# Layer 0, first batch: reciprocals for the memory's queries move to unit 1, the memory's products to units 2 and 3, and all the bit work on the codes' second half to unit 0

## The chip, the cores and the metric

The kernel runs on one core of a Trainium2 chip. The metric is the device time of one execution in microseconds (us); the median of several runs stands for a kernel. The engines have one instruction queue each and meet only at semaphores: PE (TensorE), DVE (VectorE), ACT (ScalarE), POOL (GpSimd) and SP (SyncE, which issues all the DMAs here).

## The reference, cut to what matters

Two layers; each adds an attention block and a feed-forward block to the residual `x` of shape (8, 256, 256). The change lies in layer 0, in its first two batches of eight. Layer 0's attention is a softmax attention with 32 query heads on 8 key heads, plus a read of a small fixed memory by transformed queries:

```
xn      = layernorm(x)
q, k, v = xn @ Wq.T, xn @ Wk.T, xn @ Wv.T
a_dot   = softmax(q k^T / sqrt(8)) v
sigma_q = elu(q)                                     # 4 query groups of 64 numbers per token
a_mem   = sigma_q @ memory / (sigma_q @ memory_norm)
w       = sigmoid(memory_weight)
x       = x + a_dot * (1 - w) + a_mem * w + ffn(xn)
ffn(xn) = (gelu(xn @ Wg.T) * (xn @ Wu.T)) @ Wd.T     # Wg, Wu, Wd: 4-bit codes times block scales, 2048 wide
```

The 4-bit weights are decoded on the chip. A byte with two codes is turned by shifts and masks into two bytes that are read as 8-bit floats (the "bits" below); those are multiplied with the scales, and the product is split into a high and a low part for the matmuls.

## The kernel before, in words

**Units.** Layer 0 runs as a software pipeline of units `u` from -3 (`FIRST`) on, one for each of the 64 pairs of batch and key head. Every engine walks the same list of units, and within one does, in a fixed order, its share of: the turned scores and exponentials of attention unit u, the scores and row maxima of unit u+2, the weighted values of unit u-1, the feed-forward gate and up products of m = u-1 (one of eight pieces `a` of the hidden width), and the down product of m-2. The dictionary that `schedule()` returns puts further steps of a batch (its statistics, normalisation, projections, the memory's read) at given units. All engines read the same dictionary, so moving an entry moves the step on every engine that has a part in it.

**The steps touched.** `recip0` and `recip1` make 1/(1 - tanh) parts of the elu for the two halves of the queries. On DVE (L602, L604): a tensor_scalar and a reciprocal into `q_rec`. On POOL (L331, L334): a product (semaphore `q_mul_done`) and a subtraction into `sigma` (`sigma_done`). `q_rec` lies in the same memory as `xn`, the normalised tokens. `norm` on DVE (L584) writes `xn` for batch b and waits, for b > 0, until `q_mul_done` has reached 2b. `mem` is the memory's read for one tile of 128 tokens: PE multiplies `sigma` with the memory (L848, waits for `sigma_done`), DVE takes a reciprocal, multiplies out of PSUM (L615, semaphore `mem_mul`) and adds to X (L618). `turn` transposes `xn` on PE (L825), ACT copies the high part (L421), DVE makes the low part (L588).

**One PSUM bank, `misc`.** The steps `turn`, `q`, `kv`, `v`, `mem` and `gamma` share it with the transposed maxima and with the weighted values. So PE's `steps(u)` waits ahead of the first step of a unit for `max_split` of unit u+1 (which DVE does in `split_max`, its first work of a unit), and between two steps of one unit for the DVE and ACT to have emptied the bank (`evicted`; for `mem` that is `mem_mul`). After its steps PE goes on, in order, with `scores_turned(u, 1)` (L891), `scores(u + 2, 0)` (L866), the up product (L794), `weighted(u - 1)` (L906), half of the down product (L933), `scores(u + 2, 1)` and `turn_out`.

**DVE's order in a unit.** split_max(u+1); the steps that don't use `misc` (stats, norm, recip); decoding of two weight pieces (L707) in units 0 to 5; the first gelu product (L755); the steps that use `misc`; maximum(u+2, 0) (L652); the second gelu product (L763); maximum(u+2, 1); normalised(u-1) (L671, L676); the low part of one weight piece (L712).

**POOL's order in a unit.** hidden_low(m-1) (L365); hidden(m) (L371), which waits for DVE's L763; weights_low(u+2) (L375), which waits for ACT's high part (L466); then the steps in the dictionary.

**Before the pipeline is full.** In unit -1 DVE does `decode(2)`, `decode(3)`, the memory's weights (L558 to L563), recip0, `weights_low(1)` and two of four bit operations on the second half of the codes (`nibble_bits(1, 0)` is L685 and L686, `nibble_bits(1, 1)` is L689); in unit 0 recip1, the statistics of batch 1 and the other two (L692, L695). The first half's bits are done with the same four calls in unit -3.


Of the kernel before, what the change touches and what calls it, by code (L numbers as in the profile page):

```python
# [75 lines left out]
def schedule():  # L76

    at = {}

    def put(u, *step):  # L80
        at.setdefault(u, []).append(step)

    for kind in ("stats", "norm", "turn", "q", "qlow", "kv", "qload0", "mask0", "qload1", "mask1"):
        put(FIRST, kind, 0)
    put(-1, "recip0", 0)
    put(0, "recip1", 0)
    put(0, "v", 0)
    put(1, "mem", 0)
    put(2, "mem", 1)
    put(GAMMA_AT, "gamma", 0)  # L90
    for b in range(1, BATCH):
        late = int(b == 1)
        for n, kind in ((0, "stats"), (1, "norm"), (2 + late, "turn"), (3 + late, "q"), (4 + late, "qlow"), (4 + late, "qload0"), (4 + late, "kv"),
                        (5, "mask0"), (5, "recip0"), (6, "recip1"), (8, "qload1"), (8, "mask1")):
            put(HEADS * (b - 1) + n, kind, b)
        for t in range(2):
            put(HEADS * (b - 1) + 7 + t, "mem", 2 * b + t)
        put(HEADS * (b - 1) + 9, "v", b)
    for b in range(BATCH):
        put(HEADS * b + HEADS + 1, "att", b)  # L100
        put(HEADS * b + HEADS + LAG + BEHIND, "mlp", b)
    return at


def layer0(nc, dram, keep):

    X, ident = keep["X"], keep["ident"]
    at = schedule()
    with ExitStack() as ctx:
        def sb(name, shape, dt=F32):  # L110
            return ctx.enter_context(nc.sbuf_tensor(name, shape, dt))
# [30 lines left out]
        stats = sb("stats0", [P, 2, 6])  # L142
# [41 lines left out]
        def w_exact(n):  # L184
            return w_stage[:] if n % 2 == 0 else hid_flat if n < 6 else low_front
# [10 lines left out]
        def attends(u):  # L196
            return 0 <= u < UNITS
# [114 lines left out]
        def _(pool):  # L312
# [55 lines left out]
            def hidden(m):  # L368
                pool.wait_ge(S["v1_done"], m + 1)
                pool.wait_ge(S["up_copied"], m + 1)  # L370
                pool.tensor_tensor(hid[:, m % 2, :], g[:, m % 2, :], hid[:, m % 2, :], ALU.mult).then_inc(S["hid_done"], 1)  # L371

            def weights_low(a):
                pool.wait_ge(S["w2_hi_done"], 2 * a + 1)
                pool.tensor_tensor(w_lo[:, a, 0, :], w_exact(2 * a), w_hi[:, a, 0, :].bitcast(F32), ALU.subtract).then_inc(S["w2_lo_even"], 1)  # L375
# [15 lines left out]
            for u in range(FIRST, LAST):  # L391
                m = u - LAG
                if 0 <= m - 1 < M:
                    hidden_low(m - 1)
                if 0 <= m < M:
                    hidden(m)
                if 0 <= u + 2 < PAIRS_N and u >= 0:
                    weights_low(u + 2)
                for kind, n in at.get(u, []):
                    if kind == "mask1" and u == FIRST:  # L400
                        weights_low(0)
                    step(kind, n)
                    if kind == "recip0" and u == -1:
                        weights_low(1)
                i, odd = divmod(u - SIGN_AT - 1, 2)
                if 0 <= i < PIECES and not odd:
                    signs(i)
                if 0 <= u - NEXT_AT - 2 < 4:
                    next_low(u - NEXT_AT - 2)
# [138 lines left out]
        def _(dve):  # L548
# [130 lines left out]
            def nibble_bits(half, n):  # L679

                at4 = slice(PAIRS_N // 2 * CW * half, PAIRS_N // 2 * CW * (half + 1))
                c, lo, hi, part = codes[half], low[:, at4], high[:, at4], bits[half]
                if n == 0:
                    dve.wait_ge(S[f"codes{half}"], 16)
                    dve.tensor_scalar(part, c, 2, 0x1C1C, ALU.logical_shift_left, ALU.bitwise_and).then_inc(S["dve_link"], 1)  # L685
                    dve.tensor_scalar(lo, c, 4, 0x8080, ALU.logical_shift_left, ALU.bitwise_and).then_inc(S["dve_link"], 1)  # L686
                    dve.wait_ge(S["dve_link"], linked(2))
                elif n == 1:
                    dve.tensor_tensor(lo, lo, part, ALU.bitwise_or).then_inc(S["dve_link"], 1)  # L689
                    dve.wait_ge(S["dve_link"], linked())  # L690
                elif n == 2:
                    dve.tensor_scalar(part, c, 2, 0x1C1C, ALU.logical_shift_right, ALU.bitwise_and).then_inc(S["dve_link"], 1)  # L692
                    dve.wait_ge(S["dve_link"], linked())
                else:
                    dve.scalar_tensor_tensor(out=hi, in0=c, scalar=0x8080, in1=part, op0=ALU.bitwise_and, op1=ALU.bitwise_or).then_inc(S["dve_link"], 1)  # L695
                    dve.wait_ge(S["dve_link"], linked())
# [13 lines left out]
            def weights_low(a):  # L710
                dve.wait_ge(S["w2_hi_done"], 2 * a + 2)
                dve.tensor_tensor(w_lo[:, a, 1, :], w_exact(2 * a + 1), w_hi[:, a, 1, :].bitcast(F32), ALU.subtract).then_inc(S["w2_lo_odd"], 1)  # L712
# [8 lines left out]
            for u in range(FIRST, LAST):  # L721
                m = u - LAG
                if u == FIRST:
                    for kind, n in at[u]:
                        if kind == "turn":
                            split_weights()
                        if kind != "kv":
                            step(kind, n)
                        if kind == "turn":
                            for k in range(4):  # L730
                                nibble_bits(0, k)
                    decode(0)
                    decode(1)
                    continue
                if attends(u + 1):
                    split_max(u + 1)
                for kind, n in at.get(u, []):
                    if kind not in FROM_MISC and u >= 0:
                        step(kind, n)
                i = u - SUM_AT  # L740
                if 0 <= i < PIECES:
                    dve.wait_ge(stage_sem[i % 2], 16 * (PAIRS_N // 2 + i // 2 + 1))
                    dve.tensor_reduce(asum[:, i:i + 1], stage[:, i % 2, 0:PIECE], AX_X, ALU.add, apply_absolute_value=True).then_inc(S["summed"], 1)
                if i == PIECES:
                    dve.wait_ge(S["summed"], PIECES)
                    dve.tensor_reduce(gsum[:], asum[:].rearrange("p (m n) -> p m n", m=3), AX_X, ALU.add).then_inc(S["summed"], 1)
                if u == 0:
                    nibble_bits(1, 2)
                    nibble_bits(1, 3)
                if 0 <= u < PAIRS_N - 2:  # L750
                    decode(2 * u + 4)
                    decode(2 * u + 5)
                if 0 <= m < M:
                    dve.wait_ge(S["sq_done"], m + 1)
                    dve.scalar_tensor_tensor(out=g[:, m % 2, :], in0=g[:, m % 2, :], scalar=1.0, in1=gate[:], op0=ALU.add, op1=ALU.mult).then_inc(S["u_done"], 1)  # L755
                for kind, n in at.get(u, []):
                    if kind in FROM_MISC:
                        step(kind, n)
                if attends(u + 2):
                    maximum(u + 2, 0)  # L760
                if 0 <= m < M:
                    dve.wait_ge(S["t_done"], m + 1)
                    dve.scalar_tensor_tensor(out=g[:, m % 2, :], in0=g[:, m % 2, :], scalar=1.0, in1=gate[:], op0=ALU.add, op1=ALU.mult).then_inc(S["v1_done"], 1)  # L763
                if attends(u + 2):
                    maximum(u + 2, 1)
                if u == FIRST + 1:
                    weights_low(0)
                if attends(u - 1):
                    normalised(u - 1)
                if u == -1:  # L770
                    decode(2)
                    decode(3)
                    memory_weights()
                    for kind, n in at[u]:
                        step(kind, n)
                    weights_low(1)
                    nibble_bits(1, 0)
                    nibble_bits(1, 1)
                if 0 <= u < PAIRS_N - 2:
                    weights_low(u + 2)  # L780
                if 0 <= u - NEXT_AT - 1 < KC:
                    next_centred(u - NEXT_AT - 1)
# [1233 lines left out]
```

## Time and profile before

| | us |
|---|---|
| median of 3 runs | 831.69 |
| lowest, highest | 831.38, 834.46 |
| the profiled execution's own time | 834.6 |
| its span, first to last instruction | 832.6 |
| mean granted TensorE clock | 0.955 |

Shares of the span that the engines are busy: PE 89%, DVE 75%, ACT 56%, POOL 51%. Layer 0 takes the first 600 us and some more, layer 1 the rest.

In the timeline a row is: start in us from the span's start, duration in us, engine, line, operation, output<-input with shapes, how many instructions were merged, and in brackets how long the engine was idle before it and who released it. A duration includes time in which the instruction was held back after its start. Ends of matmuls are modelled.

### The profile page before, as it was taken

The numbers are of one execution on the slowest core, as the hardware profiler recorded it, in microseconds if no ns is written. First come the engines' busy times: TensorE is split into PE (matmuls) and PEld (weight loads), VectorE is DVE, ScalarE is ACT, GpSimd is POOL, SyncE is SP. The second block draws the span as 40 slices with busy tenths as digits, with TensorE's granted clock in tenths as the row PEclk, the third lists the DMA queues.
The fourth block names the chain that finished last, engine by engine and source line by source line (L and its number), as shares of the span: only waits on it lengthen the run. The fifth ranks groups of instructions, "written<-read, shape, count | busy, mean of one in ns | idle before, by whom it ended". The sixth has DMA issues, their size and how long they took to land. (4 is left out here: it accounts for less than half of the span.)

```text
span 832.6 us, 15164 instructions
## 1 busy us (share of the span) xinstructions
PE 740.0 (89%) x5602; PEld 636.9 (76%) x5602; DVE 623.2 (75%) x1095; ACT 467.6 (56%) x746; POOL 424.4 (51%) x369
## 2 busy tenths in 40 slices
PE   3268799999999999999999999999977899999873
PEld 2256678888888888888888888888866677877773
DVE  6989878787687776767768777767346698999965
ACT  4246646655665665665566556657676656665410
POOL 2344354354346567757634524445627386584732
PEclk9569999999999999999999999999989999999985
DMA  5111121112011010101100000020110000000000
GB/s 159 29 40 40 39 78 37 36 48 59 2 33 33 24 46 21 48 27 40 34 3 21 20 3 21 4 96 3 58 35 0 1 1 26 1 1 26 1 26 25
DMA packets 22108, 25.89 MB, mean 31 GB/s; under 512 B 4498, under 2 KB 17170, under 8 KB 22036
## 3 DMA queue, kind: packets, MB, share of 16 engines
q1 hardware_dynamic: 22036, 24.93, 10.5%
q8 instruction: 45, 0.74, 0.4%
q14 instruction: 27, 0.22, 0.1%
HBM read 14.83 MB, written 3.28 MB: 22 GB/s over the span
## 5 line engine op out<-in xcount | busy, mean ns | idle before, releaser
L652 DVE TENSOR_REDUCE neg_max<-s_pair 128x4 f32<-128x1024 f32 x127 | 155.0, 1220 | 75.6 <-PE s_pair L866 75.3
L474 ACT ACTIVATE probs<-t_pair 128x1024 f32<-128x1024 f32 x128 | 131.2, 1025 | 136.4 <-PE t_pair L891 136.1
L371 POOL TENSOR_TENSOR hid<-g,hid 128x512 f32<-128x512 f32 x64 | 82.1, 1282 | 177.9 <-DVE g L763 144.8
L365 POOL TENSOR_TENSOR hid_lo<-hid,hid_hi 128x512 fp32r<-128x512 f32 x64 | 85.5, 1335 | 82.9 <-ACT hid_hi L497 82.8
L866 PE MATMUL s_pair<-K,Q 96*128 96x256 f32 x508 | 85.0, 291 | 15.6 <-DVE neg_max L652 9.3
L866 PEld LDWEIGHTS s_pair<-K,Q 96*128 96x128 f32 x508 | 75.8, 195 | 24.2 <-issue 8.1
L891 PE MATMUL t_pair<-Q,K 104*128 104x512 f32 x256 | 86.2, 418 | 0.3 <-DMA Q<-max_parts 0.3
L933 PE MATMUL down<-hi,hid_hi 128*128 128x256 f32 x256 | 83.9, 328 | 0.8 <-POOL hid_lo L365 0.8
L906 PE MATMUL misc<-probs,V 128*32 128x256 f32 x1024 | 69.4, 389 | 3.4 <-DVE kc L608 2.6
L933 PE MATMUL down<-lo,hid_hi 128*128 128x256 f32 x256 | 71.5, 279 | 0.0
L933 PE MATMUL down<-hi,hid_lo 128*128 128x256 f32 x256 | 71.2, 278 | 0.0
L933 PEld LDWEIGHTS down<-hi,hid_hi 128*128 128x128 f32 x256 | 48.0, 187 | 26.9 <-issue 24.7
L1124 POOL TENSOR_TENSOR rows<-rows,par 128x512 f32<-128x512 f32 x24 | 32.9, 1373 | 63.6 <-DVE rows L1598 46.5
L1770 PE MATMUL lbank<-lo,hi 128*128 128x512 f32 x192 | 51.2, 410 | 10.5 <-DVE l_hid L1569 9.3
L794 PE MATMUL gate<-xn_hi,hi 128*128 128x256 f32 x256 | 57.3, 305 | 0.0
L508 ACT ACTIVATE g<-g 128x512 f32<-128x512 f32 x64 | 40.1, 627 | 29.7 <-DVE g L755 29.7
L755 DVE SCALAR_TENSOR_TENSOR g<-g,gate 128x512 f32<-128x512 f32 x64 | 42.7, 668 | 18.0 <-ACT g L500 17.8
L1717 PE MATMUL lbank<-hi,lo 128*128 128x512 f32 (+1 forms) x192 | 51.0, 367 | 2.4 <-ACT lo L1315 2.3
L1770 PEld LDWEIGHTS lbank<-lo,hi 128*128 128x128 f32 x192 | 35.7, 193 | 22.4 <-DVE l_hid L1569 14.0
L794 PE MATMUL up<-xn_hi,hi 128*128 128x256 f32 x256 | 52.2, 286 | 0.0
L794 PE MATMUL up<-xn_lo,hi 128*128 128x256 f32 x256 | 51.9, 285 | 0.0
L794 PE MATMUL up<-xn_hi,lo 128*128 128x256 f32 x256 | 51.8, 284 | 0.0
(260 smaller groups left out, 1956.2 us busy)
## 6 DMA issues: line engine op xcount, KB each, us to landing
stage<-in_ternary SPq DMA_DIRECT2D x18, 256.0 KB, 2.8
Q<-q_hi SPq DMA_DIRECT2D x64, 64.0 KB, 2.0
stage<-in_scales SPq DMA_DIRECT2D x8, 384.0 KB, 3.4
X<-in_x SPq DMA_DIRECT2D x8, 256.0 KB, 4.2
Q<-q_lo SPq DMA_DIRECT2D x32, 64.0 KB, 2.0
Q<-max_parts SPq DMA_DIRECT2D x128, 4.0 KB
out<-X SPq DMA_DIRECT2D x8, 256.0 KB, 2.1
signs<-w_stage SPq DMA_DIRECT2D x9, 128.0 KB, 1.8
```

The lines of the kernel that those rows point to most:

```text
L365: pool.tensor_tensor(hid_lo[:, m % 2, :, :].rearrange("p a n -> p (a n)"), hid[:, m % 2, :], hid_hi[:, m % 2, :, :].rearrange("p a n -> p ...
L371: pool.tensor_tensor(hid[:, m % 2, :], g[:, m % 2, :], hid[:, m % 2, :], ALU.mult).then_inc(S["hid_done"], 1)
L474: act.activation(probs[:, u % 2, th, :], t_pair[:], ACT.Exp, scale=SCALE).then_inc(S["probs_done"], 1)
L652: dve.tensor_reduce(neg_max[:, u % 2, 4 * jp:4 * jp + 4], score_banks(u, jp)[:].rearrange("p (s n) -> p s n", n=SEQ), AX_X, ALU.max, negat ...
L755: dve.scalar_tensor_tensor(out=g[:, m % 2, :], in0=g[:, m % 2, :], scalar=1.0, in1=gate[:], op0=ALU.add, op1=ALU.mult).then_inc(S["u_done" ...
L794: mm = pe.matmul(out, lhs[a][k], rhs[b][k], start=(n == 0), stop=(n == 3 * KC - 1))
L866: mm = pe.matmul(score_banks(u, jp)[:, 512 * j + SEQ * s:512 * j + SEQ * s + SEQ], Q[0:KROWS, quad, 2 * jp + j, P * s:P * s + P], K[0:KROW ...
L891: mm = pe.matmul(t_pair[:, 512 * jp:512 * jp + 512].rearrange("p (j n) -> p j n", j=2), K[rows, quad, hq, P * th:P * th + P], Q[rows, quad ...
L906: mm = pe.matmul(misc[32 * j:32 * j + 32, 0:SEQ], V[:, th, h, :], probs[:, u % 2, th, SEQ * j:SEQ * j + SEQ], start=(th == 0), stop=(th == ...
L933: mm = pe.matmul(down[:, D * t:D * t + D], h[:, m % 2, n, P * t:P * t + P], w[:, a, n, 2 * D:3 * D], start=(a == 0 and t == 0 and n == 0 a ...
L1717: mm = pe.matmul(dst, lhs[a](k), rhs[b](k), start=(first and n == 0), stop=(last and n == 3 * KC - 1))
L1770: mm = pe.matmul(banks[bank][:], w[:, k, P * c:P * c + P], x[:, k, :], start=(n == 0), stop=(n == 3))
```

## The change

```diff
@@ schedule()
     for kind in ("stats", "norm", "turn", "q", "qlow", "kv", "qload0", "mask0", "qload1", "mask1"):
         put(FIRST, kind, 0)
-    put(-1, "recip0", 0)
-    put(0, "recip1", 0)
     put(0, "v", 0)
-    put(1, "mem", 0)
-    put(2, "mem", 1)
+    put(1, "recip0", 0)
+    put(1, "recip1", 0)
+    put(2, "mem", 0)
+    put(3, "mem", 1)
     put(GAMMA_AT, "gamma", 0)
     for b in range(1, BATCH):
         late = int(b == 1)
-        for n, kind in ((0, "stats"), (1, "norm"), (2 + late, "turn"), (3 + late, "q"), ...
+        for n, kind in ((0, "stats"), (1 + late, "norm"), (2 + late, "turn"), (3 + late, "q"), ...
@@ gpsimd
                 for kind, n in at.get(u, []):
                     if kind == "mask1" and u == FIRST:
                         weights_low(0)
                     step(kind, n)
-                    if kind == "recip0" and u == -1:
-                        weights_low(1)
+                if u == -1:
+                    weights_low(1)
@@ vector
                 if u == 0:
-                    nibble_bits(1, 2)
-                    nibble_bits(1, 3)
+                    for k in range(4):
+                        nibble_bits(1, k)
...
                     decode(2)
                     decode(3)
                     memory_weights()
-                    for kind, n in at[u]:
-                        step(kind, n)
                     weights_low(1)
-                    nibble_bits(1, 0)
-                    nibble_bits(1, 1)
```

Both halves of the reciprocals of batch 0 (DVE and POOL) now stand in unit 1, `mem` of tile 0 in unit 2, `mem` of tile 1 in unit 3 ahead of `turn` of batch 1, `norm` of batch 1 in unit 2, and DVE's four bit operations on the second half of the codes in unit 0. The set of instructions is the same.

## Rows read from the trace of the kernel before

**Rows 1.** Busy us by stage, per engine (instructions), then granted clock, DMA share, GB/s.

```profile
60.00:80.00 20.00, 15.08 (x127) 12.52 (x126) 18.74 (x27) 11.98 (x19) 10.21 (x7) 1.00 0.15 41
...
120.00:140.00 20.00, 20.00 (x178) 17.22 (x171) 15.03 (x29) 10.26 (x17) 9.14 (x8) 1.00 0.14 36
```

**Rows 2.** Waits of DVE, 20 to 90 us: total us, times, longest.

```profile
DVE neg_max L652 <- PE s_pair L866: 5.9, 6, 1.9
```

**Rows 3.** Timeline, unit -3: bits of the codes' first half, POOL idle.

```profile
9.50 0.55 DVE L685 TENSOR_SCALAR probs<-probs 128x1536 uint16<-128x1536 uint16 x1
...
10.55 0.96 DVE L689 TENSOR_TENSOR X<-X,probs 128x1536 uint16<-128x1536 uint16 x1
```

**Rows 4.** Timeline, unit -1, of DVE, ACT and POOL.

```profile
30.02 0.85 ACT L466 ACTIVATE hi<-w_stage 128x768 fp32r<-128x768 f32 x1 [6.61 <-DVE w_stage L707]
...
31.42 0.28 DVE L602 TENSOR_SCALAR xn<-queries 128x256 f32<-128x256 f32 x1
...
31.74 1.75 DVE L604 RECIPROCAL xn<-xn 128x256 f32<-128x256 f32 x1
...
33.41 0.90 DVE L712 TENSOR_TENSOR lo<-hid,hi 128x768 fp32r<-128x768 f32 x1
...
34.22 1.08 DVE L685 TENSOR_SCALAR probs<-probs 128x1536 uint16<-128x1536 uint16 x1
...
35.84 2.11 POOL L375 TENSOR_TENSOR lo<-w_stage,hi 128x768 fp32r<-128x768 f32 x1
...
36.33 2.44 DVE L689 TENSOR_TENSOR X<-X,probs 128x1536 uint16<-128x1536 uint16 x1
```

**Rows 5.** Timeline, end of unit 0 to start of unit 2.

```profile
48.22 0.73 POOL L331 TENSOR_TENSOR queries<-queries,xn 128x256 f32<-128x256 f32 x1
...
49.03 0.73 POOL L334 TENSOR_TENSOR queries<-queries 128x256 f32<-128x256 f32 x1
...
51.75 0.71 DVE L584 TENSOR_SCALAR xn<-X,mv,rstd 128x256 f32<-128x256 f32 x2
...
54.90 0.18 DVE L613 RECIPROCAL a_rec<-misc 128x4 f32<-128x4 f32 x1
...
55.92 1.22 DVE L652 TENSOR_REDUCE neg_max<-s_pair 128x4 f32<-128x1024 f32 x1
...
59.06 1.82 POOL L375 TENSOR_TENSOR lo<-w_stage,hi 128x768 fp32r<-128x768 f32 x1
...
59.48 2.22 DVE L712 TENSOR_TENSOR lo<-X,hi 128x768 fp32r<-128x768 f32 x1
...
60.84 1.98 POOL L365 TENSOR_TENSOR hid_lo<-hid,hid_hi 128x512 fp32r<-128x512 f32 x1
...
62.14 1.50 DVE L707 SCALAR_TENSOR_TENSOR w_stage<-X,stage 128x768 f32<-128x768 fp8e4 x1
...
62.26 0.71 PE L848 MATMUL misc<-mem,queries 128*128 128x130 f32 x4 [1.61 <-DVE max_parts L661]
```

**Rows 6.** Timeline, unit 3, of PE and DVE.

```profile
72.37 0.66 PE L825 MATMUL misc<-ident,xn 128*128 128x128 f32 x4 [1.61 <-DVE max_parts L661]
...
74.54 0.67 DVE L755 SCALAR_TENSOR_TENSOR g<-g,gate 128x512 f32<-128x512 f32 x1
...
75.00 0.40 PE L794 MATMUL up<-xn_lo,hi 128*128 128x256 f32 x2
...
75.87 1.07 PE L906 MATMUL misc<-probs,V 128*32 128x256 f32 x16 [0.47 <-DVE xn_lo L588]
...
78.36 1.23 DVE L652 TENSOR_REDUCE neg_max<-s_pair 128x4 f32<-128x1024 f32 x1 [0.82 <-PE s_pair L866]
```

**Rows 7.** Timeline of PE, unit 6.

```profile
107.70 0.71 PE L866 MATMUL s_pair<-K,Q 96*128 96x256 f32 x4 [1.89 <-issue]
...
110.46 1.93 PE L906 MATMUL misc<-probs,V 128*32 128x256 f32 x16
```

**Rows 8.** Windows: half a microsecond of unit 6, columns as in Rows 1.

```profile
109.50:110.00 0.50, 0.50 (x4) 0.50 (x4) 0.50 (x2) 0.00 (x0) 0.50 (x1) 0.50 0.88 309
```

More of the change, by code:

```diff
@@ L92, in schedule @@
         late = int(b == 1)
-        for n, kind in ((0, "stats"), (1, "norm"), (2 + late, "turn"), (3 + late, "q"), (4 + late, "qlow"), (4 + late, "qload0"), (4 + late, "kv"),
+        for n, kind in ((0, "stats"), (1 + late, "norm"), (2 + late, "turn"), (3 + late, "q"), (4 + late, "qlow"), (4 + late, "qload0"), (4 + late, "kv"),
                         (5, "mask0"), (5, "recip0"), (6, "recip1"), (8, "qload1"), (8, "mask1")):
```

## The prediction

> **What bounds the kernel now.** I read the busy shares by stage first, then the waits, then the timeline unit by unit. Busy time by stage [rows 1] shows two regimes: from 60 to 80 us DVE is busy 18.74 of 20 us and PE 15.08; from 120 to 140 us PE is busy for all 20.00 and DVE for 15.03. So the first units are set by DVE, later ones by PE. The waits of DVE from 20 to 90 us [rows 2] say that it stood still for 5.9 us only, each time between two row maxima that PE must serve. All engines walk the same units and are tied to each other in each, so I take it that a microsecond won or lost on DVE before unit 4 comes through to the end, one for one. The change moves work only inside units -1 to 3; I follow DVE through them.
>
> **Unit -1.** The first reciprocal step goes: from 31.42 to the end of the row that starts at 31.74 and takes 1.75 us, 2.07 us [rows 4]. Behind it stands DVE's `weights_low(1)` at 33.41. It cannot move up by as much. POOL's own `weights_low(1)` no longer waits behind its recip0 and starts when ACT has made the high part, at 30.02 + 0.85 = 30.87; it takes 1.82 us [rows 4, 5], to 32.7. Where DVE met such a POOL instruction it was held until that was over: the row at 36.33 took 2.44 us, ending 0.82 us after POOL's of 35.84 to 37.95; the same operation with POOL idle took 0.96 [rows 3, 4]. So `weights_low(1)` starts at 32.7 in place of 33.41: 0.7 us won (bounds 0.7 and 2.07).
>
> **The bits.** The first two bit operations of the second half took from 34.22 to 38.77, 4.55 us, beside POOL's recip0 and `weights_low(1)`; for the first half they took from 9.50 to 11.51, 2.01 us [rows 3, 4]. In the new unit 0 they start at some 35 us, when POOL has finished `weights_low(1)` and has nothing until the next high part. So 2.54 us are won (bounds 0 and 2.54; I take the whole). The other two cost the same where they are.
>
> The Trainium skill ("SBUF — State Buffer", Who interferes with whom) says that a VectorE instruction with two SBUF inputs and a GpSimd instruction that reads SBUF share a port, and that whoever comes first holds it for its whole length. The trace agrees: 0.82 us left after POOL's end, against 0.96 alone. By it both terms above stand as they are; it speaks against the change in unit 2 below, where four more POOL instructions come beside DVE's.
>
> **Unit 0.** The second reciprocal step goes too, 2.07 us. Split maxima of head 1 come 6 us earlier, so PE's transposes, turned scores and scores of head 2 are early, but DVE is what they wait for next, so that is worth nothing by itself. Batch 1's statistics stay. Sum to here: -0.7 - 2.5 - 2.1 = -5.3 us.
>
> **Unit 1.** Both reciprocal steps come in, +4.1 us. `norm` leaves, 51.75 to 52.39, -0.6; `mem` leaves, from 54.90 to the maximum at 55.92, -1.0 [rows 5]. DVE has no pause here that could hide them: they stand ahead of decoding, and gate, scores and up of PE are finished before DVE asks for them. SP's loads of the next scales come earlier than before and are off the path. At the end of unit 1 the new kernel is -5.3 + 4.1 - 0.6 - 1.0 = -2.8 us.
>
> **Unit 2.** This is the first place where it loses. `norm` may not write until POOL has done the product of recip1, since it writes over the reciprocals. POOL stands late: its steps come behind hidden(0), which waits for DVE's second gelu product, and behind weights_low(3). In the old times: weights_low(3) runs from 59.06 to 60.88, DVE's weights_low from 59.48, held up, to 61.70 [rows 5]. POOL's first product meets that and ends about 0.65 after it, 62.35; the next two start at the measured step of 49.03 - 48.22 = 0.81 us and end near 64.0. DVE would begin `norm` where decoding began, 62.14. It waits 1.9 us (bounds 0.5, if POOL goes ahead of DVE's weights_low, and 2.7, if it is held up twice), and `norm` itself is +0.6. The fourth POOL operation and then hidden_low(0), 1.98 us with its wait, run beside norm and two decodings; before, only the tail of hidden_low did and made one of them 1.50 us. I add 0.7 (0 to 1.3; the nearest row is that decoding at 62.14, which ran beside hidden_low until 62.82, 0.7 us). The page's rule would add 1.3, everything in turn, and make the sum 0.6 larger. PE's `mem` waits for `sigma_done`, near 65.1 in place of 62.26, but DVE has the norm and the decodings to do meanwhile; that is hidden. Sum: +3.2, the kernel stands at +0.4.
>
> **Unit 3.** Here is the largest term. PE now has two steps on `misc`: `mem` of tile 1, then `turn` of batch 1. Between them PE waits for DVE to have multiplied out of `misc`. DVE comes to that only after decoding and the first gelu product. The gelu product starts at 74.54 and ends at 75.21 [rows 6]; reciprocal and product of `mem` are 0.6 of its 1.0 us, so the bank is free at 75.75. Queued on PE behind that wait are turn, turned scores, scores of u+2 and the up product: from 72.37 to 75.40 before, 3.03 us, all of it in DVE's decoding time. Now they start at 75.75 and end at 78.8; the weighted values follow, where before they followed at 75.87 [rows 6]. Then half of down, and the scores that DVE's second maximum at 78.36 waited for already (0.82 us idle). Nothing of the 2.9 us is covered: DVE has `turn`, one maximum and one product, 2.6 us, and then stands. `mem`'s 1.0 us on DVE lies inside. +2.9 us (bounds 2.0, from the 0.82 idle and DVE's own extra 1.0, and 3.9).
>
> **TensorE's clock.** PE will stand still for some 4.4 us in unit 2 (before `mem`; it was 1.61) and for 1.6 and 2.9 us in unit 3. In unit 6 of the old trace PE was idle for 1.89 us before row 107.70, and soon after it the granted clock was 0.50, 1.2 GHz [rows 7, 8]; the weighted values then took 1.93 in place of 1.07 us [rows 6, 7]. Unit 3's chain on PE (3.0 us, and 2.5 from 75.87 to 78.36) is now on the path, so half clock in it costs: 0.9 for the weighted values alone, 5.5 if all of it ran at half clock. I take 1.5, since such a spell covered only part of unit 6. The Trainium skill ("TensorE: Matmul & The Clock Gate", Part 1) says that the clock is gated by how busy the array has been; by that rule the fall comes in both units, as by the row.
>
> **Sum.** -2.8 + 3.2 + 2.9 + 1.5 = +4.8 us. The profiled execution took 834.6 us (span 832.6), 2.9 above the median 831.69 of the runs shown, and at their top; the terms are differences of a few units and I put them on the median: 836.5 us. What a measurement of this kernel can tell from no change is about 0.5%, 4.2 us: below 827.5 and above 835.9.
>
> **Rivals.**
> - *The waits are shorter and the clock stays up.* POOL gets in ahead of DVE's weights_low, PE's gaps fall so that no half clock comes into unit 3: -2.8 + 0.6 + 0.5 + 2.0 to 2.9 + 0 = +0.3 to +1.5, about 832.9. For it: at 60 to 62 and 71 to 72 us PE was idle 1.61 us without harm [rows 5, 6]. Against: the new gaps are longer. Chance 0.3.
> - *The early start is kept* (the other side). The bits freed from POOL and PE's early start give 5.3 us before unit 1, and unit 3 refills from it: if weighted values and down in unit 3 were not what DVE waits for (it has batch 1's low part and a longer low-weights step to do), only norm's wait remains: -5.3 + 2.5 + 0.6 + 0.5 = -1.7, 830; and the half clock in unit 6, which hangs on where PE's gap falls, may vanish, up to -1.4 more by the 0.9 of one row and the 2.0 around it. It decides faster only where unit 3 adds under 1 us. Against it: PE walks in order, so 3.03 us of work is really behind `mem_mul`. Chance 0.13, of which 0.08 is beyond 0.5%.
> - *Twice held.* Half clock already in unit 2: PE's mem to up, some 3 us, doubles and pushes unit 2's weighted values behind DVE as well, +1 to +2, and most of unit 3 at half clock too, 2.9 + 4.5: -2.8 + 3.2 + 1.5 + 7.4 = +9.3, 841. Chance 0.12.
> - *The change does less than it says*: the terms cancel within a microsecond because the units before 4 leave slack later (DVE idle between maxima). Chance 0.05.
>
> The forecast has the remaining 0.4, from +3 to +7 us; three quarters of it lies above 4.2 us. Slower: 0.3 + 0.12 and some of the first rival's top, 0.48. Faster 0.08. Same 0.44. The likeliest case's own range is 834.7 to 838.7; with the others 830.5 to 840.5.
>
> **What would show it.** In the new profile: row L685 of the second half near 35 us at 0.55 us; a wait of DVE's L584 on POOL's L331 of some 1.9 us in unit 2; a wait of PE's L825 on DVE's L615 of 2 to 3 us in unit 3, and behind it a maximum L652 idle for over 2 us; half clock near 60 to 75 us. The prediction is wrong if L584 starts without a wait, if PE reaches `weighted` in unit 3 as early against DVE as before, or if a later stage gives the difference back.

## The result, and the profile after

| | median us | lowest to highest | ratio to the kernel before, 95% interval |
|---|---|---|---|
| before (6 runs beside it) | 831.6 | 831.29 to 834.46 | |
| changed (6 runs) | 837.81 | 835.91 to 840.79 | 1.0058 (1.0033 to 1.0083) |

The change costs 6.2 us by the medians; 4.8 was forecast (836.5). The ratio of the table, which is worked out from all the runs and is not the quotient of the medians, makes it 4.8 us (2.7 to 6.9). The profiled execution of the changed kernel took 840.79 us, its span is 838.8 (before 832.6).

The best ruler in both traces is DVE's first instruction of a unit, the split maximum L659. The time from one such row to the next is the length of the unit. These rows of the changed kernel open units 2, 3 and 4 (timeline, DVE):

```profile
60.65 0.27 DVE L659 CAST max_parts<-misc 8x128 fp32r<-8x128 f32 x1
...
73.99 0.27 DVE L659 CAST max_parts<-misc 8x128 fp32r<-8x128 f32 x1
...
88.74 0.27 DVE L659 CAST max_parts<-misc 8x128 fp32r<-8x128 f32 x1
```

Unit 2 is 73.99 - 60.65 = 13.34 us long, unit 3 14.75. All lengths, worked out like this from the traces:

| unit | -1 | 0 | 1 | 2 | 3 | 4 | 5 | 6 | 7 |
|---|---|---|---|---|---|---|---|---|---|
| before | 13.93 | 12.43 | 10.39 | 10.11 | 9.72 | 11.25 | 13.08 | 10.25 | 8.38 |
| changed | 8.76 | 12.54 | 12.60 | 13.34 | 14.75 | 11.25 | 13.08 | 10.22 | 8.37 |
| sum of differences | -5.17 | -5.06 | -2.85 | +0.38 | +5.41 | +5.41 | +5.41 | +5.38 | +5.37 |

So by these two traces, one execution of each kernel, the change is worth +5.4 us, all of it made in units -1 to 3 and none given back after. The rest of the 6.2 us between the two spans is not its doing: the first split maximum stands at 24.87 us before and at 26.75 after, 1.9 us later, with the same instructions ahead of it (PE's first projection started 0.6 us later, and from the start of PE's kv product to ACT's copy of it it took 3.0 us in place of 1.7, its rows 0.63 us each in place of 0.40); e5, e6, e7 and e9 below, in which that code is the same too, have it between 24.6 and 26.3; near 325 us the trace of before has half clock that the other has not, 1.5 us the other way; 0.4 us are in layer 1.

**The stage** (busy time, columns as in [rows 1]):

```profile
60.00:80.00 20.00, 12.36 (x75) 10.15 (x74) 16.48 (x26) 7.44 (x11) 9.72 (x8) 0.84 0.08 20
```

DVE is busy for 16.48 us where it was 18.74 [rows 1], PE for 12.36 in place of 15.08, and the granted clock fell from 1.00 to 0.84: both engines stand more, so it is waits that were added, not work. (The two windows hold different parts of the units, so they show the kind of the loss and not its size.)

**What DVE waits for now** (waits of DVE, 20 to 90 us, columns as in [rows 2]):

```profile
DVE neg_max L652 <- PE s_pair L862: 7.1, 6, 3.5
DVE xn L584 <- POOL queries L331: 1.7, 1, 1.7
DVE xn_lo L588 <- ACT xn_hi L421: 1.4, 1, 1.4
```

Against 5.9 us for maxima alone [rows 2] there are now 7.1, and two waits that were not there. PE's waits from 60 to 80 us name the other side:

```profile
PE misc L821 <- DVE a_mem L615: 2.7, 1, 2.7
PE misc L844 <- POOL queries L334: 2.5, 2, 1.5
```

**Units -1 and 0** (timeline, DVE and POOL; answers to [rows 3, 4]):

```profile
32.83 1.81 POOL L375 TENSOR_TENSOR lo<-w_stage,hi 128x768 fp32r<-128x768 f32 x1 [6.82 <-ACT hi L466]
...
33.10 1.61 DVE L563 TENSOR_SCALAR mem<-mem,mw 128x128 f32<-128x128 f32 x1
...
34.64 0.94 DVE L712 TENSOR_TENSOR lo<-hid,hi 128x768 fp32r<-128x768 f32 x1
...
36.95 0.53 DVE L685 TENSOR_SCALAR probs<-probs 128x1536 uint16<-128x1536 uint16 x1
...
37.98 0.96 DVE L689 TENSOR_TENSOR X<-X,probs 128x1536 uint16<-128x1536 uint16 x1
```

POOL's weights_low starts right after ACT's high part, DVE's L563 is held up by it (1.61 in place of 0.28 us) and its weights_low follows. L685 takes 0.53 and L689 0.96 us, as with POOL idle in unit -3 [rows 3]; before the change they took 1.08 and 2.44 [rows 4].

**Unit 2** (timeline, the same engines and PE; answers to [rows 5]):

```profile
59.87 1.44 POOL L331 TENSOR_TENSOR queries<-queries,xn 128x256 f32<-128x256 f32 x1
...
62.07 0.72 POOL L331 TENSOR_TENSOR queries<-queries,xn 128x256 f32<-128x256 f32 x1
...
62.26 0.46 PE L844 MATMUL misc<-mem,queries 128*128 128x130 f32 x2 [1.53 <-POOL queries L334]
...
62.90 2.13 DVE L584 TENSOR_SCALAR xn<-X,mv,rstd 128x256 f32<-128x256 f32 x2 [1.66 <-POOL queries L331]
...
63.65 0.66 PE L844 MATMUL misc<-mem,queries 128*128 128x130 f32 x2 [0.93 <-POOL queries L334]
...
64.94 0.95 DVE L707 SCALAR_TENSOR_TENSOR w_stage<-X,stage 128x768 f32<-128x768 fp8e4 x1
...
70.34 1.23 DVE L652 TENSOR_REDUCE neg_max<-s_pair 128x4 f32<-128x1024 f32 x1 [0.24 <-PE s_pair L862]
```

DVE's `norm` at 62.90 has waited 1.66 us for POOL's second product, and takes 2.13 us for its two instructions (0.71 before), held up by POOL's fourth operation and by hidden_low. PE's two products for `mem` come at 62.26 and 63.65, waiting for `sigma_done`. The granted clock is at its lower level from 63.8 to 67.3 us, but DVE's second maximum waits for only 0.24 us, so the end of this unit is DVE's.

**Unit 3** (timeline of PE and DVE; answers to [rows 6]):

```profile
74.62 0.71 PE L844 MATMUL misc<-mem,queries 128*128 128x130 f32 x4 [1.61 <-DVE max_parts L661]
...
77.59 0.42 DVE L615 TENSOR_TENSOR a_mem<-misc,a_rec 128x256 f32<-128x256 f32 x1
...
78.07 1.12 PE L821 MATMUL misc<-ident,xn 128*128 128x128 f32 x4 [2.73 <-DVE a_mem L615]
...
82.83 0.63 PE L790 MATMUL up<-xn_lo,hi 128*128 128x256 f32 x2
...
83.39 1.50 PE L902 MATMUL misc<-probs,V 128*32 128x256 f32 x16
...
86.29 1.22 DVE L652 TENSOR_REDUCE neg_max<-s_pair 128x4 f32<-128x1024 f32 x1 [3.53 <-PE s_pair L862]
```

PE does `mem` at 74.62 and stands for 2.73 us until DVE has multiplied out of the bank (77.59 + 0.42). Turn to the end of up takes from 78.07 to 83.46, 5.4 us in place of 3.03, since the granted clock is at its lower level, 1.2 GHz, from 77.5 to 84.3 us. A row of the windows within it (columns as in [rows 1]):

```profile
78.50:79.00 0.50, 0.50 (x5) 0.50 (x4) 0.00 (x0) 0.00 (x0) 0.00 (x0) 0.50 0.00 0
```

The weighted values follow at 83.39 and DVE's second maximum at 86.29, after an idle time of 3.53 us (0.82 before).

### The profile page after: what moved, and what is told of

Same layout as the page of the kernel before. It is cut to its first block and busy times, and to the rows that moved or that the text cites. A ratio compares the mean times of both kernels' runs of the same rounds, so it can differ in the third digit from the quotient of the medians.

```text
span 838.8 us, 15164 instructions
## 1 busy us (share of the span) xinstructions
PE 748.1 (89%) x5602; PEld 644.5 (77%) x5602; DVE 621.9 (74%) x1095; ACT 468.3 (56%) x746; POOL 424.9 (51%) x369
## 5 line engine op out<-in xcount | busy, mean ns | idle before, releaser
L862 PE MATMUL s_pair<-K,Q 96*128 96x256 f32 x508 | 86.8, 295 | 17.9 <-DVE neg_max L652 12.5
L862 PEld LDWEIGHTS s_pair<-K,Q 96*128 96x128 f32 x508 | 77.7, 199 | 26.8 <-DVE neg_max L652 8.8
```

Source lines behind the costliest of these rows:

```text
L862: mm = pe.matmul(score_banks(u, jp)[:, 512 * j + SEQ * s:512 * j + SEQ * s + SEQ], Q[0:KROWS, quad, 2 * jp + j, P * s:P * s + P], K[0:KROW ...
```

## The experiments

For each run the unit lengths come from its trace; each is from one traced execution. They agree between traces to 0.05 us wherever the code is the same and no spell of half clock lies differently (it does in unit 3, table behind e5, and in units 5 and 6), so they tell more than the whole times, of which one kernel's lie up to 6 us apart. The kernel before had a median of 832.62 us beside e1 to e4, 833.57 beside e5 to e8 and 833.45 beside e9. In the diffs "..." stands for lines left out.

| | units -1, 0, 1, 2, 3 | sum of 5 | median us | ratio to before, 95% |
|---|---|---|---|---|
| before | 13.93, 12.43, 10.39, 10.11, 9.72 | 56.6 | | |
| changed | 8.76, 12.54, 12.60, 13.34, 14.75 | 62.0 | 837.81 | 1.0058 (1.0033 to 1.0083) |
| e1 mem in the down bank | 8.75, 12.54, 12.61, 13.38, 10.74 | 58.0 | 834.16 | 1.0021 (1.0007 to 1.0034) |
| e2 filler in unit 3 | 8.76, 12.54, 12.60, 13.36, 11.97 | 59.2 | 837.34 | 1.0049 (1.0032 to 1.0065) |
| e3 mem first | 8.76, 12.53, 12.61, 13.36, 11.43 | 58.7 | 835.37 | 1.0029 (1.0012 to 1.0046) |
| e4 own reciprocals | 8.75, 12.54, 12.59, 13.86, 14.18 | 61.9 | 837.38 | 1.0059 (1.0036 to 1.0083) |
| e5 mem late | 13.92, 12.42, 9.39, 10.11, 14.03 | 59.9 | 837.30 | 1.0045 (1.0029 to 1.0062) |
| e6 bits | 9.35, 14.50, 10.39, 10.12, 9.72 | 54.1 | 831.12 | 0.9970 (0.9955 to 0.9985) |
| e7 gaps | 9.42, 14.30, 10.84, 10.12, 9.72 | 54.4 | 831.75 | 0.9974 (0.9961 to 0.9988) |
| e8 own reciprocals, filler | 8.76, 12.54, 12.60, 11.71, 13.61 | 59.2 | 836.01 (1 run) | |
| e9 bits, first in the pause | 9.43, 13.43, 10.40, 10.13, 9.70 | 53.1 | 830.73 | 0.9966 (0.9948 to 0.9983) |

The ratios to the kernel before agree with the sums to 0.7 us, but for e2: +4.1 us (2.7 to 5.4) by its ratio, +2.6 by its trace.

### e1: the memory's products in another bank

```diff
 # PE, step "mem"
+                    if b == 1:
+                        pe.wait_ge(S["mem_mul"], 1)
-                        mm = pe.matmul(misc[:, ...
+                        mm = pe.matmul((down if b < 2 else misc)[:, ...
 # PE, evicted
-                elif kind == "mem":
+                elif kind == "mem" and n >= 2:
 # PE, down_product
+                    if m == 0:
+                        pe.wait_ge(S["mem_mul"], 2)
 # DVE, step "mem"
-                    am = misc[:, ...
+                    am = (down if b < 2 else misc)[:, ...
```

> The changed kernel, but the memory's two products of batch 0 go to the PSUM bank of the down product (unused until the end of unit 3), so PE need not wait for DVE between them and turn in unit 3. The unit lengths here are from one first split-maximum row (L659) to the next. Theory (the wait for the shared bank is the cost): unit 3 falls from 14.75 to some 10.7 us, that is the 9.72 of the kernel before and 1.0 for the step on DVE; whole time 4 us below the changed kernel. Rival A (half clock is the cost, the wait is not): unit 3 stays over 12.7. Rival B (DVE's added work is the cost): unit 3 stays at 13.7 or more.

Unit 3 took 10.74 us. The timeline of PE and DVE:

```profile
74.82 0.60 PE L821 MATMUL misc<-ident,xn 128*128 128x128 f32 x4
...
78.78 1.07 PE L904 MATMUL misc<-probs,V 128*32 128x256 f32 x16 [0.97 <-DVE xn_lo L588]
...
81.26 1.23 DVE L652 TENSOR_REDUCE neg_max<-s_pair 128x4 f32<-128x1024 f32 x1 [0.81 <-PE s_pair L864]
```

Turn follows `mem` at once, at full clock, and the whole queue behind it goes by while DVE decodes. The weighted values now wait for DVE's low part of batch 1, as before the change; what is left of unit 3 is DVE's own 1.0 us. Rival B falls: of the 5.03 us that unit 3 had gained, 4.0 hang on the shared bank. Rival A's number did not come either, but with the wait the half clock is gone too (the granted clock is 1.00 from 73.6 to 84.4 us), so what each is worth is left to e2. The run shows one thing more: here the granted clock was 0.50 up to 69.2 us, through most of unit 2, and that unit took 13.38 us where the changed kernel with its shorter spell took 13.34. Half clock costs nothing there.

### e2: the same wait, with the clock held up

```diff
                     if before:
+                        if u == 3:
+                            for n3 in range(20):
+                                pe.matmul(down[:, 0:SEQ], w_hi[:, 0, 0, 0:P], xn_hi[:, 0, 0, :], start=True, stop=True)
                         evicted(*before)
```

> The changed kernel with 20 useless matmuls of 256 columns on PE in unit 3, between the memory's product and the wait for the bank, into the still unused down bank; they take some 2.4 us of a wait of 2.73. Theory (2.0 of the 5.0 us of unit 3 are half clock after PE's pause): the granted clock stays 1.0 and unit 3 falls from 14.75 to 12.7 us. Rival (the clock costs nothing on the path): unit 3 stays at 14.7 or grows.

Unit 3 took 11.97 us, 2.8 less than without the filler; 12.7 was expected. The timeline:

```profile
74.23 2.64 PE L944 MATMUL down<-xn_hi,hi 128*128 128x256 f32 x20
...
77.22 0.66 PE L821 MATMUL misc<-ident,xn 128*128 128x128 f32 x4 [0.35 <-DVE a_mem L615]
...
80.19 1.07 PE L902 MATMUL misc<-probs,V 128*32 128x256 f32 x16
...
82.68 1.23 DVE L652 TENSOR_REDUCE neg_max<-s_pair 128x4 f32<-128x1024 f32 x1 [1.73 <-PE s_pair L862]
...
84.19 0.98 DVE L712 TENSOR_TENSOR lo<-X,hi 128x768 fp32r<-128x768 f32 x1
```

The last of these in the kernel before:

```profile
79.88 1.65 DVE L712 TENSOR_TENSOR lo<-X,hi 128x768 fp32r<-128x768 f32 x1
```

Turn begins as late against the unit's start as before (77.22 - 73.12 = 4.10, in the changed kernel 78.07 - 73.99 = 4.08), but the queue behind it is through in 2.97 us, not 5.32. DVE's second maximum stands 9.56 us into the unit (82.68 - 73.12); it was 6.63 before the change (78.36 - 71.73) and 12.30 with it (86.29 - 73.99). So up to there the queue behind the bank is worth 2.93 us and half clock 2.74. Behind it the changed kernel is 0.64 us and this one 0.68 us quicker than the kernel before: DVE's weights_low came clear of POOL's and took 0.98 us here in place of 1.65. That makes 2.93 + 2.74 - 0.64 = 5.03. The 2.93 hold the 1.0 us of DVE's own step, which e1 left in the unit. The whole times do not show the gain (837.34 us beside 837.81 for the changed kernel), and this is one trace; the table behind e5 bears it out from four others.

### e3: DVE empties the bank first

```diff
+                if u == 3:
+                    step("mem", 1)
                 if 0 <= u < PAIRS_N - 2:
                     decode(2 * u + 4)
...
-                    if kind in FROM_MISC:
+                    if kind in FROM_MISC and (u, kind) != (3, "mem"):
```

> The changed kernel, but in unit 3 DVE does its part of the memory's read for tile 1 ahead of decoding instead of after the first gelu product. Theory (PE's queue behind the bank is the cost, since DVE comes late): PE's turn starts 2 us earlier against the start of the unit, and unit 3 takes about 11.8 us in place of 14.75. Rival (DVE's order is of no account since DVE does the same work): 14 us or more, with a new wait of DVE for PE's product.

```profile
74.44 0.18 DVE L613 RECIPROCAL a_rec<-misc 128x4 f32<-128x4 f32 x1 [0.81 <-PE misc L846]
...
75.14 1.12 PE L823 MATMUL misc<-ident,xn 128*128 128x128 f32 x4 [0.74 <-DVE a_mem L615]
...
79.57 1.07 PE L904 MATMUL misc<-probs,V 128*32 128x256 f32 x16
```

Turn starts 75.14 - 73.05 = 2.09 us into the unit in place of 4.08, at the price of 0.81 us in which DVE waits for PE's product. Unit 3 took 11.43 us; 11.8 was expected. Part of it ran at half clock still (L823 1.12 us).

### e4: norm without its wait

```diff
+        q_rec0 = hid[:, 1, :].rearrange("p (c n) -> p c n", c=2)
...      # DVE and POOL, recip: q_rec0 for batch 0, the old place for the others
-                    if b > 0:
+                    if b > 1:
                         dve.wait_ge(S["q_mul_done"], 2 * b)
```

> The changed kernel, but the reciprocals of batch 0 are written to a free part of hid, not over xn, and norm of batch 1 does not wait for POOL's products. Theory (the wait of norm is a term of its own): unit 2 falls from 13.34 to about 11.9 us. Rival (POOL's and DVE's instructions take turns whatever the wait): norm and the decodings are held up instead, and unit 2 stays at 13 us.

Unit 2 took 13.86 us, more than with the wait. My theory falls as I had put it. The rival's hold-ups are there (two decodings of 1.48 us in place of 0.95), but they did not end the unit either. The timeline:

```profile
60.35 1.13 DVE L586 TENSOR_SCALAR xn<-X,mv,rstd 128x256 f32<-128x256 f32 x2
...
62.14 1.32 POOL L336 TENSOR_TENSOR queries<-queries 128x256 f32<-128x256 f32 x1
...
63.51 0.80 PE L847 MATMUL misc<-mem,queries 128*128 128x130 f32 x2 [1.57 <-POOL queries L336]
...
64.19 0.67 DVE L758 SCALAR_TENSOR_TENSOR g<-g,gate 128x512 f32<-128x512 f32 x1
...
68.51 1.33 PE L905 MATMUL misc<-probs,V 128*32 128x256 f32 x16
...
70.54 1.23 DVE L655 TENSOR_REDUCE neg_max<-s_pair 128x4 f32<-128x1024 f32 x1 [2.67 <-PE s_pair L865]
```

The wait of `norm` is gone, and DVE comes to its first gelu product 4.36 us into the unit (64.19 - 59.83), 1.67 earlier than in the changed kernel (66.68 - 60.65 less 4.36). But then DVE is idle for 2.67 us before its second maximum. PE's second product for `mem` starts at 63.51, held by POOL's fourth operation (1.32 us, itself held up), and PE works at half clock from 62.3 to 69.1 us, twice as long as in the changed kernel (63.8 to 67.3). So two chains stand behind unit 2, DVE's by `norm` and PE's by `sigma_done` and half clock; taking away one shows the other, here 0.5 us later than in the changed kernel.

### e8: e4, with PE kept busy in its pauses

```diff
                     for c in range(2):
+                        if b == 0:
+                            for n3 in range(10):
+                                pe.matmul(down[:, 0:SEQ], w_hi[:, 0, 0, 0:P], xn_hi[:, 0, 0, :], start=True, stop=True)
                         pe.wait_ge(S["sigma_done"], 2 * (b // 2) + c + 1)
```

> The changed kernel with reciprocals in a free part of hid, as in the run before in which norm's wait was gone and unit 2 took 13.86 us all the same, and with ten useless matmuls of 256 columns ahead of each of PE's two products for the memory in unit 2. Theory (PE's half clock after its pause took the gain): the clock stays up after the pause and unit 2 takes 12.3 us or less. Rival (sigma_done comes late because POOL's last subtraction is held up, and PE's queue behind it is what ends unit 2, at any clock): 13.3 us or more.

```profile
62.13 1.44 PE L848 MATMUL down<-xn_hi,hi 128*128 128x256 f32 x10
...
63.76 0.49 PE L850 MATMUL misc<-mem,queries 128*128 128x130 f32 x2 [0.20 <-POOL queries L336]
...
66.57 1.07 PE L908 MATMUL misc<-probs,V 128*32 128x256 f32 x16
...
68.35 1.23 DVE L655 TENSOR_REDUCE neg_max<-s_pair 128x4 f32<-128x1024 f32 x1 [0.49 <-PE s_pair L868]
```

PE's second product comes as late as before (63.76 - 60.05 = 3.71 us into the unit, 3.68 in e4), the clock stays up, and the weighted values start 2.8 us after it in place of 5.0. Unit 2 took 11.71 us. This settles e4, by one execution: `sigma_done` is as late as there, and it was half clock on PE that took the gain.

### e5: the memory's products late, nothing else

```diff
-    put(1, "mem", 0)
-    put(2, "mem", 1)
+    put(2, "mem", 0)
+    put(3, "mem", 1)
```

> The kernel before with one part of the change: the memory's product for tile 0 in unit 2 and for tile 1 in unit 3, all else as before (recip0 in unit -1, recip1 in unit 0, norm in unit 1). Unit lengths are from one first split-maximum row (L659) to the next; before they are 13.93, 12.43, 10.39, 10.11, 9.72 us for units -1 to 3. Theory (the parts add up): units -1, 0 and 2 unchanged, unit 1 9.4 (one mem step less), unit 3 14.7 as in the changed kernel; +4.0 us in all. Rival (unit 3 is long only because unit 2 was disturbed): unit 3 below 12.

```profile
76.23 1.12 PE L825 MATMUL misc<-ident,xn 128*128 128x128 f32 x4 [2.73 <-DVE a_mem L615]
...
83.76 1.23 DVE L652 TENSOR_REDUCE neg_max<-s_pair 128x4 f32<-128x1024 f32 x1 [2.85 <-PE s_pair L866]
```

9.39 and 14.03 us for units 1 and 3, units -1, 0 and 2 as before, +3.3 in all; 4.0 was expected. Unit 3's share does not need a disturbed unit 2. It is 0.7 us shorter than in the changed kernel with the same instructions in unit 3, since the spell of half clock lay otherwise (74.0 to 80.9 us here, and ended within the up product). This part and e6's make +0.8 of the +5.4; the rest, 4.6 us, would be the moves of the reciprocals and of `norm`, which no run made alone.

Five traces have these instructions in unit 3 and the same wait for the bank: turn starts 4.08 to 4.10 us into the unit in all of them. They differ in where the half clock lies (windows of a quarter of a microsecond):

| | half clock, us into unit 3 | of it behind the start of turn | second maximum, us into the unit | later than in e2, per us of half clock behind turn's start |
|---|---|---|---|---|
| changed | 3.5 to 10.3 | 6.24 | 12.30 | 0.44 |
| e4 | 2.2 to 9.1 | 4.97 | 11.74 | 0.44 |
| e5 | 1.9 to 8.7 | 4.64 | 11.62 | 0.44 |
| e8 | 0.9 to 7.8 | 3.68 | 11.19 | 0.44 |
| e2 | none | 0 | 9.56 | |

A straight line through the upper four rows comes to 9.6 us at no half clock at all, where e2 has 9.56. So half clock over the pause costs nothing, and each microsecond of it over the queue behind the bank costs 0.44. In these four traces that is 1.6 to 2.7 us, by where the spell happened to lie.

### e6: all the bits in unit 0, nothing else

```diff
                 if u == 0:
-                    nibble_bits(1, 2)
-                    nibble_bits(1, 3)
+                    for k in range(4):
+                        nibble_bits(1, k)
...
                     weights_low(1)
-                    nibble_bits(1, 0)
-                    nibble_bits(1, 1)
```

> The kernel before with one other part: all four bit operations on the second half of the codes in unit 0, all else as before. Theory (POOL's neighbourhood made two of them cost 4.55 in place of 2.01 us): units -1 and 0 together take 26.36 - 2.5 = 23.9 us, at worst 24.8, since recip1's first instruction can now meet POOL's recip0; the whole time falls by 1.6 to 2.5 us. Rival (the early start was worth it, not the bits): 26 us or more.

```profile
37.39 0.53 DVE L685 TENSOR_SCALAR probs<-probs 128x1536 uint16<-128x1536 uint16 x1
...
38.42 0.96 DVE L689 TENSOR_TENSOR X<-X,probs 128x1536 uint16<-128x1536 uint16 x1
```

Units -1 and 0 took 23.85 us, units 1 to 3 are unchanged: this part alone is a gain of 2.5 us, and the kernel is faster than the one before, by 0.3% of the whole time.

### e7: DVE's pauses filled

```diff
-                    nibble_bits(1, 2)
-                    nibble_bits(1, 3)
+                    for k in range(1, 4):
+                        nibble_bits(1, k)
...
+                if u == -1:
+                    nibble_bits(1, 0)
+                if u == 0:
+                    step("recip1", 0)
                 if attends(u + 2):
                     maximum(u + 2, 1)
```

> The kernel before with DVE's work of units -1 and 0 in another order: the first bit operation (L685, L686) of the second half between the two maxima of unit -1, where DVE idled 1.32 us, the other three in unit 0, and recip1 between the two maxima of unit 0, where it idled 1.38 us. Theory (DVE sets these units, so filled pauses and untroubled bits are won one for one): units -1 and 0 together take 26.36 - 2.5 - 1.05 - 1.38 = 21.4 us, the later units are unchanged, the whole time 4.9 us below the kernel before. Rival (something else ends these units as soon as DVE is quicker): 23.5 us or more, or the gain is given back in units 1 to 4.

The two units took 23.72 us and unit 1 0.45 more: not the 21.4 of my theory, and both numbers of the rival came (over 23.5, and a part given back in unit 1). Timeline of DVE and POOL:

```profile
37.12 2.62 POOL L375 TENSOR_TENSOR lo<-w_stage,hi 128x768 fp32r<-128x768 f32 x1
...
38.10 2.06 DVE L692 TENSOR_SCALAR probs<-probs 128x1536 uint16<-128x1536 uint16 x1
...
44.87 1.00 DVE L602 TENSOR_SCALAR xn<-queries 128x256 f32<-128x256 f32 x1
```

Without recip1 ahead of them the bits came 2 us sooner and met POOL's weights_low: L692 took 2.06 in place of 0.56 us, and L602 in the second pause 1.00 in place of 0.29. DVE's weights_low of unit 0, now beside POOL's recip1, took 1.44 in place of 0.95. These three, 2.7 us, are more than the 2.3 us by which the theory missed. In unit 1 `norm` waits 0.35 us for POOL's part of the statistics, which come behind recip1: that one is a new bound.

### e9: the first bit operation in the pause, the rest behind recip1

```diff
                 if u == 0:
-                    nibble_bits(1, 2)
-                    nibble_bits(1, 3)
+                    for k in range(1, 4):
+                        nibble_bits(1, k)
...
+                if u == -1:
+                    nibble_bits(1, 0)
                 if attends(u + 2):
                     maximum(u + 2, 1)
```

> The kernel before with the first bit operation of the second half between the two maxima of unit -1 and the other three in unit 0; recip1 stays where it was. Theory (in the run with the filled pauses the gain went to instructions of DVE that were held up by POOL, L692 and L602, not to a new bound): with recip1 and the statistics ahead of them the bits start when POOL has finished, units -1 and 0 together take 23.85 - 1.05 = 22.8 us, and the time is 3.5 us below the kernel before. Rival (DVE's pauses can't be filled because the next maximum is late whatever it does): 23.8 us, as with the bits in unit 0 alone.

```profile
27.81 0.54 DVE L685 TENSOR_SCALAR probs<-probs 128x1536 uint16<-128x1536 uint16 x1
...
29.27 1.22 DVE L652 TENSOR_REDUCE neg_max<-s_pair 128x4 f32<-128x1024 f32 x1 [0.45 <-PE s_pair L866]
...
39.95 0.56 DVE L692 TENSOR_SCALAR probs<-probs 128x1536 uint16<-128x1536 uint16 x1
```

22.86 us for the two units, L692 0.56 us again, and 0.45 us left of the pause of 1.32. By its trace it is the shortest of all kernels here; its median is 830.73 us beside 833.45 for the kernel before on the same chip, ratio 0.9966 (0.9948 to 0.9983), by the traces 3.5 us less. Whether it beats e6 by its 1.0 us the whole times can't tell.

## Why the prediction was right

By its own steps, forecast against the trace:

- **Units -1 and 0**: -5.3 forecast, -5.06 measured. That POOL's weights_low would hold DVE back, and that the bits would cost 2.0 us, came out (e6: -2.5 alone). But the instruction that was held is L563, ahead of weights_low in DVE's queue (1.61 us in place of 0.28); weights_low itself took its 0.94 us. That came to the same end.
- **Unit 1**: -2.8 forecast at its end, -2.85 measured. That it is so near is in part luck: the unit alone was forecast at +2.5 and took +2.21, and the 0.3 us cancel the 0.24 missed before.
- **Unit 2**: +3.2 forecast, +3.23 measured. The wait of `norm` was 1.66 for 1.9, the hold-ups beside it 0.9 for 0.7 (norm 2.13 in place of 0.71, less the decoding of 1.50 that now took 0.95). The step that failed was in what I called hidden: PE's `mem`, late by `sigma_done`, of which I wrote "that is hidden". It was hidden only by DVE's own wait. With `norm` freed (e4) PE's chain ended the unit, 0.5 us later still, and half clock was what made it long (e8, 13.86 to 11.71). PE's pause was also smaller than the 4.4 us of the forecast: 1.53 and 0.93 us, with a product between. The rival of half clock already in unit 2 was half right: it came (63.8 to 67.3 us), and cost nothing that DVE's wait did not cost already, as e1's unit 2 shows.
- **Unit 3**: 2.9 for the queue behind the bank and 1.5 for the clock, 4.4 in all; measured 5.03. The mechanism is shown by e1 and e3, the split by e2: 2.93 us for the queue, 2.74 for half clock, and 0.64 that DVE won back behind its second maximum, which I had not seen. The term that was mis-sized is the clock's, 1.5 for 2.74: I had taken the one spell of unit 6 as the measure, but here it lay over the whole chain, from 77.5 to 84.3 us, over turn, scores and up. The 2.74 is this trace's: with the same instructions in unit 3 the clock cost 1.6 to 2.2 us in e4, e5 and e8. So the size of this term hangs on where the spell falls, which the forecast had no means to tell, and that the sum of +4.8 lies as near as it does to +5.4 is in part luck.
- **One for one to the end**: +5.41 after unit 3, +5.37 after unit 7. It holds.

The rival in which the early start is kept falls with the same table: it needed unit 3 to add under 1 us, and the unit added 5.03. The rival with shorter waits and full clock did not happen either; the top of its range, +1.5, is about where e1 stands (58.0 against 56.6 us), by taking the wait away.

The Trainium skill's rule on the shared port ("SBUF — State Buffer", Who interferes with whom) was borne out in both directions: moving the bits away from POOL gave 2.5 us, and POOL's instructions beside DVE's took 0.9 back in unit 2. The prediction told it for instructions with two SBUF inputs; the rows show instructions with one held as well (L563, L685, L692, `norm`). In e7 the same holding up took a gain that no count of DVE's idle time would have shown.

## What to carry to other kernels

Two steps that share one PSUM bank in one unit put everything PE has queued behind them on the path of the engine that empties the bank; ask what is queued, not how long the step is. A pause that is made on TensorE can be paid twice, as a wait and as half clock in the work that follows it, but only where that work is what another engine waits for: 2.74 us in unit 3, nothing in unit 2. And not every pause brings it: in unit 3 of the kernel before, after 1.61 us [rows 6], the clock stayed at 1.00 [rows 1]. And when an instruction is moved on DVE, look at what POOL does at the new time: the same instruction costs 0.56 or 2.06 us.

## What was not expected of the hardware

Useless matmuls in a pause can be worth having: twenty of them, some 2.6 us of PE, made unit 3 2.8 us shorter (e2), twenty in unit 2 2.15 us (e8, against e4), both by unit lengths of one trace each; the whole times of e2 do not show it.

Unit lengths repeat to 0.05 us from one trace to the next, except where spells of half clock lie differently: units 5 and 6, where all eleven kernels are equal, took 13.08 + 10.2 us in four traces, 13.08 + 8.7 in four and 14.92 + 7.34 in three. In e6 (13.07 + 8.71) the granted clock was 1.00 from 98 to 118 us; in the kernel before (13.08 + 10.25) it was 0.50 from 108.9 to 112.2. That is up to 1.5 us. The start (first split maximum at 24.6 to 26.8 us) is up to 2.2; a unit near 325 us is 1.5 us longer in four of the eleven traces; and from the last split maximum to the end it takes 244.8 us in e1, 247.5 in e4 and 248.6 to 249.4 in the others. Together this is of the size of the 6 us by which the runs of the kernel before lie apart; that it is their cause was not tested.
